# Turning a running maximum back in transpose mode, and building a one-hot block from eight or four operations with a scalar per partition

## The reference, cut to what matters

```python
deg = jax.ops.segment_sum(jnp.ones((src.shape[0],), x.dtype), dst, num_segments=n)
agg_sum = jax.ops.segment_sum(x[src], dst, num_segments=n)
...
hp = jax.nn.relu(x @ W_pool + b_pool)
agg_max = jax.ops.segment_max(hp[src], dst, num_segments=n)
...
score = jnp.exp(jnp.clip(score.sum(-1, keepdims=True), -5.0, 5.0))
msg = V_h[src_idx] * score
wV = jax.ops.segment_sum(msg, dst_idx, num_segments=N)
Z = jax.ops.segment_sum(score, dst_idx, num_segments=N)
```

## Time and profile before

| | before |
|---|---|
| median of 3 runs | 4438.12 us (4435.52 to 4441.56) |
| the profiled execution | 4438.06 us, span 4436.3 us |
| PE busy | 4362.1 us, 98% of the span |
| PEld busy | 3921.0 us, 88% |
| POOL busy | 3123.4 us, 70% |
| DVE busy | 2229.0 us, 50% |
| ACT busy | 1420.3 us, 32% |
| granted TensorE clock, mean | 0.989 of full speed |
| chain of work that ended last | PE 96%, its largest line L1019 with 17% |

### The profile page before, as it was taken

The page is one execution under the profiler, slowest core; times in us unless marked ns, Lnnn a source line. Parts: engine busy times, 40 slices in busy tenths (PEclk is TensorE's granted clock), DMA queues, the critical chain, the costliest instruction groups (busy, mean ns, idle before and its releaser), DMA issues.

```text
span 4436.3 us, 109751 instructions
## 1 busy us (share of the span) xinstructions
PE 4362.1 (98%) x32762; PEld 3921.0 (88%) x32762; DVE 2229.0 (50%) x5236; ACT 1420.3 (32%) x3823; POOL 3123.4 (70%) x3252
## 2 busy tenths in 40 slices
PE   8999999999999999999989999999999999999996
PEld 7989899999999898989858999999999999999996
DVE  5444444444444444444455555555555555555556
ACT  3333333333333333333243333333333333333333
POOL 7776776777766767667517777777777777777774
PEclk9999999999999999999989999999999999999997
DMA  3111111111111111111124444444444444444442
GB/s 88 38 36 36 36 36 36 36 37 36 37 36 36 37 36 36 36 36 37 27 63 119 116 116 116 116 117 114 117 116 116 116 117 115 116 117 117 116 116 78
DMA packets 209077, 333.35 MB, mean 75 GB/s; under 512 B 73181, under 2 KB 156824, under 8 KB 208952
## 3 DMA queue, kind: packets, MB, share of 16 engines
q0 software_dynamic: 129040, 238.05, 22.6%
q1 hardware_dynamic: 80008, 94.94, 6.9%
HBM read 325.49 MB, written 7.24 MB: 75 GB/s over the span
## 4 chain that ended last, share of the span: by engine, by line
PE 96%; DVE 1%; issue 1%; POOL 1%; ACT 0%; DMA 0%; SPq 0%; POOLq 0%; ACTq 0%; DVEq 0%
PE bank L1019 17%; PE bank L1143 9%; PE bank L1121 9%; PE bank L1129 9%; PE bank L1138 8%; PE bank L988 8%; PE bank L999 8%; PE bank L1160 8%; PE bank L1010 6%; PE bank L1028 6%; PE bank L990 4%; PE bank L1152 1%; POOL kvg L394 1%; PE bank L1069 1%; PE bank L1070 1%
## 5 line engine op out<-in xcount | busy, mean ns | idle before, releaser
L394 POOL DMA_INDIRECT kvg<-in_x_dram,idx x1613 | 1538.0, 954 | 648.4 <-issue 638.7
L394 POOL DMA_INDIRECT kvg<-kv_table,idx x1613 | 1557.6, 966 | 509.0 <-issue 459.9
L1019 PE MATMUL bank<-ident,scan 96*128 96x96 f32 x3232 | 832.0, 400 | 0.0
L667 DVE TENSOR_TENSOR acc<-acc,bank 97x64 f32 (+1 forms) x808 | 177.5, 220 | 1244.7 <-PE bank L1010 949.9
L1019 PEld LDWEIGHTS bank<-ident,scan 96*128 96x128 f32 x3232 | 787.3, 328 | 0.0
L551 ACT COPY eaC<-bank 96x512 f32<-96x512 f32 x404 | 234.7, 581 | 1119.2 <-PE bank L1121 1108.7
L473 ACT COPY scanE<-bank 128x384 f32<-128x384 f32 x404 | 193.1, 478 | 1225.5 <-PE bank L1019 1225.5
L1028 PEld LDWEIGHTS bank<-S,scanE 128*96 128x96 f32 x3232 | 339.6, 165 | 216.0 <-issue 214.0
L657 DVE TENSOR_TENSOR_SCAN scan<-keepC,scan,bank 96x512 f32<-96x512 bf16 x404 | 513.1, 1270 | 0.0
L642 DVE TENSOR_TENSOR S<-iotaW,rel 128x512 f32<-128x512 f32 (+1 forms) x808 | 445.8, 552 | 25.5 <-issue 25.5
L1143 PE MATMUL bank<-qwin,scan 64*128 64x96 f32 x3232 | 456.0, 281 | 0.0
(11 more groups left out here) (125 smaller groups left out, 5038.4 us busy)
## 6 DMA issues: line engine op xcount, KB each, us to landing
ea<-in_edge_attr_dram SPq DMA_DIRECT2D x402, 192.0 KB, 2.5
kvg<-in_x_dram,idx POOLq DMA_INDIRECT x1613, 2.5
kvg<-kv_table,idx POOLq DMA_INDIRECT x1613
kv_table<-stage SPq DMA_DIRECT2D x6, 672.0 KB, 3.3
stage<-counts_row SPq DMA_DIRECT2D x1, 2352.0 KB, 12.9
xN<-in_x_dram SPq DMA_DIRECT2D x6, 336.0 KB, 3.3
out_dram<-xN SPq DMA_DIRECT2D x6, 336.0 KB
src_all<-in_src_groups_dram SPq DMA_DIRECT2D x1, 804.0 KB
```

The costliest lines, as they stand in the source:

```text
L394: pool.indirect_dma_start(out=to[:, r, j, :], out_offset=None, in_=table, in_offset=bass.IndirectOffsetOnAxis(ap=idx[:, r, j:j + 1], axis= ...
L1019: last = pe.matmul(bank[4 + b][:, j * D:(j + 1) * D], scan[:, b, j:GE:J], ident[0:D, 0:D], start=True, stop=True)
```

## The change

Two edits. First, the one-hot block of a group is no longer made by one `tensor_tensor` that compares two broadcast views (512 elements a partition in stage 1, 256 in stage 2), but by one `tensor_scalar` for each of the eight (or four) blocks of 64, which compares `iotaW` with one number per partition, the column of `rel` that belongs to the block. The waits and the semaphore are as before; the last of the eight raises it. Second, `back` uses `pe.transpose` in place of a matmul with the identity: the same operands and the same place in PSUM, but in TensorE's transpose mode, which the kernel has at L1008 already.

```diff
@@ one_hot (DVE)
                 dve.wait_ge(s_used, freed(i, r, R))
-                dve.tensor_tensor(S[:, r % R, 0:cols * J, :], iotaW[:, :].unsqueeze(1).to_broadcast([P, cols * J, W]),
-                                  rel[:, bass.ds(i * R + r, 1), 0:cols, :].rearrange("p a b j -> p (a b j)")
-                                  .unsqueeze(2).to_broadcast([P, cols * J, W]),
-                                  ALU.is_equal).then_inc(s_made, 1)
+                for n in range(cols * J):
+                    last = dve.tensor_scalar(S[:, r % R, n, :], iotaW[:, :],
+                                             rel[:, bass.ds(i * R + r, 1), n // J, n % J:n % J + 1]
+                                             .rearrange("p a b -> p (a b)"), None, ALU.is_equal)
+                last.then_inc(s_made, 1)
@@ back (PE)
                     for j in range(J):
-                        last = pe.matmul(bank[4 + b][:, j * D:(j + 1) * D], scan[:, b, j:GE:J], ident[0:D, 0:D],
-                                         start=True, stop=True)
+                        last = pe.transpose(bank[4 + b][:, j * D:(j + 1) * D], scan[:, b, j:GE:J], ident[0:D, 0:D])
                     last.then_inc(s_back, 1)
```

## The result

The changed kernel takes **4268.61 us** (median of 4 runs, 4268.01 to 4270.08), the kernel before 4439.34 (4 runs): ratio 0.9617, 95% interval 0.96 to 0.9633. That is 171 us less, inside the range, 19 us under the forecast of 4288.

The account below looks back on a forecast made before the run. PE bounds both stages, with GpSimd close behind; in stage 1 GpSimd's gathers would become the bound. 150 us less in stage 1 and 0 elsewhere, from 4438.06, gives 4288 us; range 4262 to 4350.

Parts of the forecast that it names:

- The mechanism: Stage 1: PE's 5.41 us a group falls below GpSimd's 5.00, so GpSimd bounds; stage 2 stays at 5.08; 70%.
- The signs that the prediction named: Profile after: 1616 `back` records, PE waiting about 0.5 us a group, gathers 1.25 to 1.28 us apart, last at 2030 to 2080.
- The end of stage 1: Last gather starts at 2055 us, lands 2.5 later, then 12 us of tail: 2069.5 in place of 2219.5.
- The price of the port: Delay of GpSimd's gathers by the eight comparisons' claims on the port shared with VectorE: 0.06 us a group.
- The lower bound, 0: Low end of the gathers' delay by the eight comparisons, 0 us a group; the upper bound was 0.62.
- The block before is in the way too, 0.69 us at a time: Remark that the old single one-hot operation also holds the port against gathers, 0.69 us at a time; not priced.
- The block takes 1.39 us, not 1.25: Stage 1's eight comparisons on VectorE: 7 x 0.15 + 0.2 = 1.25 us, against 0.69 before.
- The loop through PE, VectorE and ScalarE: Stage 1's loop of scan, copies, matmuls and one-hot block: 8.3 us for two steps, 4.2 a step, so DVE doesn't bound.
- one operation of 0.55 us too many ahead of the message: Stage 2: a product, two more operations of 0.55 us and the message end at about 3011.25; cover 0.98 us, need 0.24.
- More delay on GpSimd: Rival: gathers delayed 0.1 to 0.35 us a group, some in stage 2 too; 4310 to 4420 us, say 4360; 14%.
- a block that shuts it out: Rival: the eight comparisons keep GpSimd out without a gap, stage 1 at 5.62 us a group; about 4570 us, slower; 7%.
- The clock: Rival: PE's clock falls because PE now waits half a microsecond in each group; 4300 to over 5000 us; 4%.

Follow-up runs that it names:

- `back_only`: The changed kernel with the one-hot block again made by the old single operation, only the running maximum's transposes in transpose mode: 4335.89 us, ratio 0.9776 against the kernel before.
- `eight_tt`: The changed kernel with the same eight and four comparisons in two-tensor form, the position spread over 64 elements: 4274.45 us, ratio 0.9637 against the kernel before.
- `immediate`: The changed kernel with each comparison against a constant in place of the position, so the block is not the one-hot: 4291.77 us.
- `stage2_tr`: The changed kernel with stage 2's eight turning matmuls (attention values and one-hot) in transpose mode as well: 5305.63 us, ratio 1.1964 against the kernel before.

## Why the prediction was right, and where its terms were off

**The mechanism held.** PE bound stage 1; `back` in transpose mode took it under GpSimd's 5.00 us a group; GpSimd became the bound, PE's waits for `kvg` are in the chain, and stage 2's step stayed at 5.08. The signs that the prediction named came too: 1616 records of `back`, the last gather at 2033 us, no longer waits of GpSimd. PE's waits were 0.77 us a group and not 0.5, so PE's own step is 4.2 us and not 4.46. The end of stage 1 was put at 2069.5 us and is 2049.4, 20.1 us earlier; this is the miss of 19 us.

**The price of the port was the mis-sized term.** I took 0.06 us a group (1.265 us a gather); 1.252 was measured. 1592 x 0.013 = 20.7 us, and the first gather of the row starts 1.1 us earlier. Against that the tail, from the last gather's start to the end of stage 1, took 2049.4 - 2033.4 = 16.0 us and not 14.5. Together 20.3, as found but for rounding. The lower bound, 0, was nearly right. I argued from single operations that a gather "waits at most one operation, 0.2 us", and that one start and one second half a group meet the block. In the trace of the loop gathers that start in the block are hardly longer at all (0.948 against 0.945 us in the mean); it is VectorE's comparisons that give way, from 0.249 to up to 0.5 us. That the term came out near nothing is in part luck: the same eight short pieces in the two-tensor form, without register instructions, held a gather to the block's end 25 times of 26, and I had no row on either.

**What I saw and didn't price.** "The block before is in the way too, 0.69 us at a time" stands in the prediction as a remark. It is worth 67 us: a step of the kernel of before that costs nothing while PE binds costs 0.16 us a group as soon as GpSimd does. My sum came out right since it compared the new block with a GpSimd that nothing disturbs. For `back` alone the same sum gives 4288 less the port's 24 us, which is what I expected of `back_only`, and it is 4336.

The block takes 1.39 us, not 1.25, because of the scalar per partition and not, as I reckoned, of the register instruction. The loop through PE, VectorE and ScalarE needs 4.46 us a group and not 4.2. GpSimd's 5.00 covers all three. In stage 2 I counted one operation of 0.55 us too many ahead of the message; its end at about 3011.25 us is right.

**The rivals.** More delay on GpSimd (14%), a block that shuts it out (7%): neither. What the second feared does happen, but in another kernel: the written-out steps of `eight_tt`. The block of `immediate` costs 0.08 us a group, an eighth of that rival's 0.62, and by another way. The clock: no fall between 100 and 2000 us; but my 4% for a clock that stays down names what eight transposes a group did in stage 2 (`stage2_tr`).

## What to carry to other kernels

Two edits may be worth 0 and 100 us alone and 171 together; test each with the other in place.

## What the runs showed of the hardware

- A gather of 128 rows (an indirect DMA on GpSimd) that starts while an operation with two SBUF inputs runs ends 0.82 us after that one does; a 0.69 us operation made it up to 1.47 us long. In the gather's second half the same operation did no harm and took none (0.942 and at most 0.694 us), while comparisons with a constant held the gather to 0.12 us after their end.
- Eight operations of the same kind and the same total work, 0.135 us apart, added 0.011 us a group with a register instruction ahead of each, and held 25 gathers of 26 to the end of the eighth without.
- A comparison of 64 fp32 elements costs VectorE 0.163 us in a row with a scalar per partition, 0.135 with a second tensor in its place, 0.102 with a constant (0.249, 0.217 and 0.183 us each when timed singly).
- Shorter intervals on VectorE can cost more overall: the 0.90 us block (a constant) delayed the gathers over six times as much as the 1.39 us one (a scalar per partition), 0.08 against 0.012 us a group.
- With all eight turning matmuls of a stage 2 group in transpose mode the granted clock stayed at 0.50 from 2183 us to the end of the stage, with PE without a pause; with four it fell and came back (0.98).
